# Experts 2 to 7 block by block: split second product, token weights by DMA broadcast, sums in PSUM

## What is computed

```python
# xf: 2080 x 128 (normalised), 8 experts, hidden size 256
probs = softmax(xf @ Wr.T + br)
top2_prob, top2_idx = top_k(probs, 2)
comb = zeros((n, 8)).at[arange(n)[:, None], top2_idx].add(top2_prob)
h = gelu(einsum('nd,edh->enh', xf, W1) + b1)        # first product
o = einsum('enh,ehd->end', h, W2) + b2              # second product
y = einsum('ne,end->nd', comb, o)
out = hidden + y
```

## Time and profile before

| | before |
|---|---|
| three runs | 258.67, 258.99, 262.17 us; median 258.99 us |
| the profiled execution | 259.49 us, of which the profile's span is 257.7 us |
| PE busy | 239.3 us, 93% of the span |
| DVE busy | 154.9 us |
| ACT busy | 132.3 us |
| POOL busy | 62.7 us |

### The profile page before, as it was taken

The page is one execution under the profiler, slowest core; times in us unless marked ns, Lnnn a source line. Parts: engine busy times, 40 slices in busy tenths (PEclk is TensorE's granted clock), DMA queues, the critical chain, the costliest instruction groups (busy, mean ns, idle before and its releaser), DMA issues.

```text
span 257.7 us, 6442 instructions
## 1 busy us (share of the span) xinstructions
PE 239.3 (93%) x2527; PEld 204.4 (79%) x2527; DVE 154.9 (60%) x460; ACT 132.3 (51%) x435; POOL 62.7 (24%) x92
## 2 busy tenths in 40 slices
PE   2899998999998899888989999999999999999993
PEld 2646564799776666677878899799999999999993
DVE  1575888864768899996467749625150606052553
ACT  2452148852299899990057893452617080807000
POOL 8833113095006455567031300000000000000000
PEclk9999999999999999999999999999999999999999
DMA  5980000000005152091000000000000000000015
GB/s 145 326 208 3 1 0 0 3 1 3 3 0 123 45 119 50 3 294 34 5 6 0 3 0 0 3 0 4 0 0 3 1 3 0 0 3 0 0 33 137
DMA packets 11366, 10.05 MB, mean 39 GB/s; under 512 B 1423, under 2 KB 10107, under 8 KB 11208
## 3 DMA queue, kind: packets, MB, share of 16 engines
q1 hardware_dynamic: 9264, 8.74, 12.9%
q10 hardware_dynamic: 1528, 0.54, 0.8%
q0 software_dynamic: 544, 0.35, 0.6%
HBM read 7.52 MB, written 2.11 MB: 37 GB/s over the span
## 4 chain that ended last, share of the span: by engine, by line
PE 61%; POOL 11%; DVE 11%; issue 10%; DMA 4%; SPq 1%; ACT 1%; DVEq 0%; POOLq 0%
PE banks L1157 57%; POOL region_e L417 5%; DMA region_a<-in_x 4%; POOL w_lo L472 2%; POOL rstd L364 2%; DVE stb L796 2%; DVE stats L778 1%; DVE top L915 1%; DVE stb L879 1%; POOL region_d L424 1%; PE banks L1357 1%; DVE h L769 1%; PE banks L1498 1%; PE banks L1305 1%; ACT stb L641 1%
## 5 line engine op out<-in xcount | busy, mean ns | idle before, releaser
L1147 DVE SCALAR_TENSOR_TENSOR KT<-banks,vbd,KT 128x128 f32<-128x128 f32 (+1 forms) x136 | 38.0, 344 | 54.2 <-PE banks L1157 53.7
L630 ACT ACTIVATE region_d<-banks,vecs 128x416 f32<-128x416 f32 x80 | 45.4, 610 | 45.0 <-PE banks L1157 44.9
L1157 PE MATMUL banks<-w_all,region_d 128*128 128x128 f32 (+1 forms) x544 | 63.0, 275 | 0.0
L1157 PEld LDWEIGHTS banks<-w_all,region_d 128*128 128x128 f32 (+1 forms) x544 | 61.4, 187 | 1.2 <-ACT region_d L630 0.2
L606 ACT ACTIVATE region_e<-banks,ntop 128x64 f32<-128x64 f32 x128 | 38.3, 348 | 4.8 <-DVE ntop L922 4.4
L606 ACT ACTIVATION_READ_ACCUMULATOR region_e<-banks,ntop 128x1 f32 x128 | 29.9, 240 | 0.0
L1157 PE MATMUL banks<-x_hi,w_hi 128*128 128x416 f32 x80 | 29.9, 373 | 0.0
L1157 PE MATMUL banks<-x_lo,w_hi 128*128 128x416 f32 x80 | 28.2, 353 | 0.0
L1157 PE MATMUL banks<-x_hi,w_lo 128*128 128x416 f32 x80 | 28.0, 351 | 0.0
L1157 PE MATMUL banks<-kc 128*128 128x128 f32 x76 | 13.6, 307 | 4.9 <-DMA kc<-in_consts 4.9
L417 POOL TENSOR_TENSOR region_e<-region_e,rsum 128x512 f32<-128x512 f32 (+1 forms) x15 | 15.5, 1031 | 7.4 <-DVE ntop L922 5.3
(11 more groups left out here) (214 smaller groups left out, 366.4 us busy)
## 6 DMA issues: line engine op xcount, KB each, us to landing
region_a<-in_x SPq DMA_DIRECT2D x2, 512.0 KB, 5.2
region_a<-in_x SPq DMA_DIRECT2D x1, 1024.0 KB, 9.9
out<-h SPq DMA_DIRECT2D x2, 512.0 KB, 5.4
h<-out SPq DMA_DIRECT2D x4, 256.0 KB, 4.4
w_sb<-in_L_ffn_W SPq DMA_DIRECT2D x1, 1024.0 KB, 5.7
region_c<-in_L_attn_rel_v SPq DMA_DIRECT2D x2, 260.0 KB, 9.9
out<-KT SPq DMA_DIRECT2D x6, 64.0 KB, 1.8
out<-KT ACTq DMA_DIRECT2D x6, 64.0 KB, 2.0
```

What stands on the lines that cost most here:

```text
L630: a.activation(HB[:, e % 2, s, blk * FB:(blk + 1) * FB], bank[h_bank(i)][:, 0:FB], ACT.Gelu, bias=vecs[:, v:v + 1]).then_inc(S["gelu_ok"], 1)
L1147: last = v.scalar_tensor_tensor(acc[0:m, t, :], bank[out_bank(u)][0:m, i * C:(i + 1) * C], comb[0:m, t, e:e + 1], acc[0:m, t, :], op0=ALU. ...
L1157: return t_.matmul(o, l, r, start=start, stop=stop)
```

## The change

- Experts 0 and 1 stay as they are. Experts 2 to 7 run in `STEPS`: for each block of 416 tokens, the six experts in turn.
- The second product now has the weights as stationary operand, split in `w2_hi` and `w2_lo`, and the 416 tokens of the block moving, hidden values split in `y_hi` and `y_lo`: three float32r matmuls a unit. A block's twelve units (36 matmuls) add up in one PSUM bank (4 or 5).
- The token's weight goes onto the hidden values ahead of the product. For that the rows of `combT` are written to the output tensor as scratch (5 DMAs on SP), and read back to all 128 partitions (15 DMAs on SP, three for each block: a semaphore `d_wb` each).
- A unit now passes ACT twice and DVE twice: `lift` (GELU, ACT), `weigh` (product with the weights, DVE), `rounded` (high part, ACT), `rest` (low part, DVE), in rings of 4 (`lifted`, in the place of `w1_sb`) and 6 (`y_hi`, `y_lo`). PE does the second product of a step two steps behind the first (`LAG`).
- A block's sum is copied by ACT (`evac_sum`), transposed back by PE (`turn_back`, 3 or 4 tiles, and the class tokens' in the last block), and added to `acc` by DVE (`joined`). Then its output DMAs go.
- `w2_hi` is made by one ACT copy of 1536 columns, `w2_lo` by three DVE subtractions of 512.
- Buffers of attention (`h0`, `vbd`, `RVBD`, `region_e`) now share their place with those of the experts; `comb` and `combT` get a buffer of their own.

```diff
+DIRECT = 2
+STEPS = [(blk, e) for blk in range(5) for e in range(DIRECT, E)]
+LATER = 2 * len(STEPS)
+LAG = 2
+G_RING, H_RING = 4, 6
+BACK = [range(0, 3), range(3, 6), range(6, 9), range(9, 13), range(13, 16)]
...
-        UNITS += [(e, blk, s) for e in range(2, E) for blk in range(5) for s in range(2)]
+        UNITS += [(e, blk, s) for blk, e in STEPS for s in range(2)]
...
+            sp_.wait_ge(S["cT_ok"], 2)
+            for c in range(4):
+                sp_.dma_start(scratch(c * P, [[ALL, E - DIRECT], [4 * P, 4], [1, P]]),
+                              combT[32 * c + DIRECT:32 * c + E, 0:4 * P].rearrange("e (g m) -> e g m", g=4))\
+                    .then_inc(S["d_cs"], 16)
+            sp_.dma_start(scratch(TOK, [[ALL, E - DIRECT], [1, IMG]]), combT[DIRECT:E, 4 * P:4 * P + IMG])\
+                .then_inc(S["d_cs"], 16)
+            sp_.wait_ge(S["d_cs"], 16 * 5)
+            for blk in range(5):
+                b = slice(blk * FB, (blk + 1) * FB)
+                sp_.dma_start(region_c[:, :].rearrange("p (e t) -> p e t", e=4)[:, :, b],
+                              scratch(blk * FB, [[0, P], [ALL, 4], [1, FB]])).then_inc(S[f"d_wb{blk}"], 16)
+                for e in range(6, 8):
+                    sp_.dma_start(weights(e)[:, b], scratch((e - DIRECT) * ALL + blk * FB, [[0, P], [1, FB]]))\
+                        .then_inc(S[f"d_wb{blk}"], 16)
...
-            for i in range(20, 10 * E):
-                gelu(i)
+            a.activation(w2_hi[:, :], w2_all[:, DIRECT * 2 * C:E * 2 * C], ACT.Copy).then_inc(S["w2hi_ok"], 1)
...
+            def lift(u):
+
+                i = 20 + u
+                blk, e = STEPS[u // 2]
+                act.wait_ge(S["h_ps"], i + 1)
+                if u >= G_RING:
+                    act.wait_ge(S["lo_ok"], u - G_RING + 1)
+                b = V_FB1 + 2 * e + u % 2
+                a.activation(lifted(u), bank[h_bank(i)][:, 0:FB], ACT.Gelu, bias=vecs[:, b:b + 1])\
+                    .then_inc(S["gelu_ok"], 1)
+
+            def rounded(u):
+
+                act.wait_ge(S["hs_ok"], u + 1)
+                if u >= H_RING:
+                    act.wait_ge(S["y3_ps"], (u - H_RING) // 2 + 1)
+                a.activation(h_hi(u), lifted(u), ACT.Copy).then_inc(S["hi_ok"], 1)
...
+            for u in range(G_RING - 1):
+                lift(u)
+            for u in range(G_RING - 1, LATER):
+                rounded(u - G_RING + 1)
+                lift(u)
+                if u >= 16 and u % 12 == 4:
+                    evac_sum((u - 16) // 12)
...
-            for e in range(E):
-                for g, tiles in enumerate(groups(e)):
+            for e in range(DIRECT):
+                for g, tiles in enumerate(GROUPS):
...
+                if e == 0:
+                    for c in range(3):
+                        split_down(c)
...
+            def weigh(u):
+
+                blk, e = STEPS[u // 2]
+                dve.wait_ge(S["gelu_ok"], 20 + u + 1)
+                dve.wait_ge(S[f"d_wb{blk}"], 48)
+                v.tensor_tensor(lifted(u), lifted(u), weights(e)[:, blk * FB:(blk + 1) * FB], ALU.mult)\
+                    .then_inc(S["hs_ok"], 1)
+
+            def rest(u):
+
+                dve.wait_ge(S["hi_ok"], u + 1)
+                dve.wait_ge(S["hs_ok"], u + 1)
+                if u >= H_RING:
+                    dve.wait_ge(S["y3_ps"], (u - H_RING) // 2 + 1)
+                v.tensor_tensor(h_lo(u), lifted(u), h_hi(u).bitcast(F32), ALU.subtract).then_inc(S["lo_ok"], 1)
...
+            for u in range(G_RING - 1):
+                weigh(u)
+            for u in range(G_RING - 1, LATER):
+                rest(u - G_RING + 1)
+                weigh(u)
+                if u >= 20 and u % 12 == 8:
+                    joined((u - 20) // 12)
...
-            up(2, 1)
+            up(DIRECT + 1, 0)
...
             down(0, 4)
-            for blk in range(2, 5):
-                up(2, blk)
-            for e in range(1, E):
-                for g in range(len(groups(e))):
-                    down(e, g)
-                if e + 2 < E:
-                    for blk in range(5):
-                        up(e + 2, blk)
+            for g in range(5):
+                down(1, g)
+
+            def down_sum(k):
+
+                blk, e = STEPS[k]
...
+                o = bank[4 + blk % 2][:, 0:FB]
+                for s in range(2):
+                    u = 2 * k + s
+                    pe.wait_ge(S["lo_ok"], u + 1)
+                    w = slice((2 * (e - DIRECT) + s) * C, (2 * (e - DIRECT) + s + 1) * C)
+                    mm(o, w2_hi[:, w], h_hi(u), e == DIRECT and s == 0, False)
+                    mm(o, w2_lo[:, w], h_hi(u), False, False)
+                    last = mm(o, w2_hi[:, w], h_lo(u), False, e == E - 1 and s == 1)
+                last.then_inc(S["y3_ps"], 1)
...
+            for n in range(LAG, len(STEPS) + LAG):
+                if n < len(STEPS):
+                    blk, e = STEPS[n]
+                    up(e, blk)
+                if n >= 9 and n % 6 == 3:
+                    turn_back((n - 9) // 6)
+                down_sum(n - LAG)
+            turn_back(4)
```

More of the change, by code:

```diff
@@ L198, in vit_kernel @@
         KM = region_b[:, :].rearrange("p (t s) -> p t s", s=2)
+        region_e = early_sb("region_e", RING * 512)
+        xi = region_e
+        tc_ = region_e
+        SP = [region_e[:, 512 * i:512 * i + 512] for i in range(RING)]
+        vbd = early_sb("vbd", IMG * C)
+        VBD = vbd[:, :].rearrange("p (b c) -> p b c", b=IMG)
+        h0 = early_sb("h0", TOK)
+        h0v = h0[:, :].rearrange("p (t c) -> p t c", c=C)
+        RVBD = early_sb("RVBD", QC * 32)
+        RV = RVBD[:, :].rearrange("p (q s d) -> p q s d", q=QC, s=2)
         early.close()
@@ L324, in _, with scratch @@
             sp_.dma_start(w2_sb, fW2.rearrange("e (s h) d -> h e s d", s=2)).then_inc(S["d_ffn"], 16)
-            for g, tiles in enumerate(LAST[1:], 1):
-                sp_.wait_ge(S["acc_ok"], out_done(out_expert(E - 1, g)))
+            def scratch(offset, dims):
+                return bass.AP(tensor=out.tensor, offset=out.offset + offset, ap=dims)
+            sp_.wait_ge(S["d_h0q"], 64)
+            sp_.wait_ge(S["cT_ok"], 2)
[13 more added lines that the diff above has]
+                        .then_inc(S[f"d_wb{blk}"], 16)
+            for blk in range(5):
+                sp_.wait_ge(S[f"d_wb{blk}"], 48)
+            for blk, tiles in enumerate(BACK):
+                sp_.wait_ge(S["fin_ok"], blk + (1 if blk < 4 else 2))
                 tt = slice(tiles[0], tiles[-1] + 1)
-                for f in range(2):
+                for f in range(4 if blk < 4 else 2):
                     sp_.dma_start(oq[f][:, tt, :], acc[32 * f:32 * f + 32, tt, :]).then_inc(S["d_out"], 16)
-            sp_.wait_ge(S["d_out"], 16 * 2 * (len(LAST) - 1))
+            sp_.wait_ge(S["d_out"], 16 * 18)
         @block.gpsimd
@@ new lines, in rounded, with evac_sum @@
+            def rounded(u):
[3 more added lines that the diff above has]
+                a.activation(h_hi(u), lifted(u), ACT.Copy).then_inc(S["hi_ok"], 1)
+            def evac_sum(blk):
+                act.wait_ge(S["y3_ps"], 6 * blk + 6)
+                a.activation(accT[:, blk * FB:(blk + 1) * FB], bank[4 + blk % 2][:, 0:FB], ACT.Copy)\
+                    .then_inc(S["at_ok"], 1)
+            for u in range(G_RING - 1):
+                lift(u)
@@ L674, in _ @@
+            for u in range(G_RING - 1, LATER):
[3 more added lines that the diff above has]
+                    evac_sum((u - 16) // 12)
+            for u in range(LATER - G_RING + 1, LATER):
+                rounded(u)
+            evac_sum(4)
             oq = out[:, 1:QC, :].rearrange("b (t f) c -> f b t c", f=4)
-            act.wait_ge(S["acc_ok"], out_done(out_expert(E - 1, 0)))
+            act.wait_ge(S["fin_ok"], 5)
             a.dma_start(out[:, 0, :], acc[0:IMG, PAIRS, :]).then_inc(S["d_out2"], 16)
[L677 to L681, removed]
@@ L682, in _ @@
-            act.wait_ge(S["d_out2"], 16 * (2 * len(LAST) - 1))
+            act.wait_ge(S["fin_ok"], 6)
+            tt = slice(BACK[4][0], BACK[4][-1] + 1)
+            for f in range(2, 4):
+                a.dma_start(oq[f][:, tt, :], acc[32 * f:32 * f + 32, tt, :]).then_inc(S["d_out2"], 16)
+            act.wait_ge(S["d_out2"], 48)
         @block.vector
@@ L1150, in _, with joined @@
                     last.then_inc(S["acc_ok"], 1)
+                if e == 0:
[13 more added lines that the diff above has]
+                v.tensor_tensor(h_lo(u), lifted(u), h_hi(u).bitcast(F32), ALU.subtract).then_inc(S["lo_ok"], 1)
+            def joined(blk):
+                dve.wait_ge(S["tb_ps"], blk + 1)
+                dve.wait_ge(S["acc_ok"], 15)
+                o = bank[6 + blk % 2]
+                if blk == 4:
+                    v.tensor_tensor(acc[0:IMG, PAIRS, :], o[0:IMG, 3 * C:4 * C], acc[0:IMG, PAIRS, :], ALU.add)\
+                        .then_inc(S["fin_ok"], 1)
```

(43 more changed lines are left out.)

44 lines of the change are left out of this document (26 added, 18 removed).

## The result

| | before | changed |
|---|---|---|
| median of 20 runs each | 260.06 us | 258.47 us |
| profiled execution, its span | 259.49, 257.7 us | 257.97, 255.8 us |
| combT ready to PE's last matmul | 91.2 us | 88.7 us |

What follows compares the result with a forecast made beforehand. The prediction took PE to bound the kernel in the experts. Its terms (-46.8 -0.5 +34.0 +2.1 +2.2 +0.5 +1.7) summed to -6.8 us, rounded to -6.7, for a median of 252.3 us against 258.99; range 250.3 to 258.5.

## What to carry over

When work is moved onto data that a new transfer brings, cost the first piece that is waited for, not the bandwidth of the whole: a semaphore for each expert's part of the first block took 5.3 us off the stage and 1.7% off the median, where total traffic stayed the same and the first reads as slow. A broadcast read of one row to all partitions needs a price of its own, or some copies of the source. And where PE will stand, add what it pays afterwards at half clock: it fell in the waits of 4.5 to 5.5 us here and not in those of about 2 us of the other versions. Last, compare the engines' paces again for each stretch: the one with slack in the stream can be the bound at its end.

## What the runs showed of the hardware

- 128 partitions reading the same rows of 1664 bytes: 84 to 128 GB/s at full DMA share in windows of 2 us up to 175 us (changed kernel, own semaphores, block 0 alone); eight partitions to a row, with 16 copies: 285 to 306; own rows for each partition: 338 to 404. Late in the changed kernel's transfers (189 to 195 us), the shared rows moved at 279 to 327 GB/s, and with block 0 alone in the queue the blocks after it were slow again (98 to 129 from 183 to 191 us). So sharing alone does not make a read slow, and why the first blocks are the slow ones stays open.
- Granted clock: PE stood 5.5 us, and it went from 2.4 to 1.2 GHz within that time; twelve matmuls ran at 0.345 us. In the 32 executions of the two sets of the changed kernel the mean clock was 0.977 to 0.993, in 31 of them at most 0.987, and in the 18 with the identity matmuls 0.990 to 1.000, so it is no chance event. It fell as well where PE stood 4.5 us (copies) and 4.7 us (block 0 alone). PE stood about 2 us in the versions without transfers, with own semaphores and with own rows, and the clock stayed at 1.00 in their profiles.
- PE needs no useful work to keep its clock: 22 matmuls of the identity did, in both profiles with them.
- DVE, tensor_tensor of 416 float32 columns, each waiting for ACT's last: 0.58 us long and started 0.50 us apart.
